# A two-layer graph network on one core: GpSimd's adding DMAs of the message stage become plain loads by SyncE, with the adds on VectorE and TensorE

## The chip, the cores and the metric

One core of one Trainium2 chip runs the whole program. The metric is the device time of one execution in microseconds (us). Five engines work side by side, each through its own instruction stream in order: TensorE (PE in the profile, its weight loads PEld), VectorE (DVE), ScalarE (ACT), GpSimd (POOL) and SyncE (SP), which here only starts DMAs.

## The reference

There are 100,000 nodes with 64 numbers each and 25,000 edges sorted by their target `dst`, each with a source `src` and 32 numbers of its own.

```
h   = relu(layernorm(x))
# layer 1: attention over the edges of a target, then batch norm over all nodes
score = sum(h[src] * h[dst]);  a = softmax of score over the edges of one dst
agg = segment_sum((h @ W_conv + b_conv)[src] * a, dst)
r   = relu(h @ W_res + b_res)
x2  = x + batchnorm(agg + r) * gamma + beta
# layer 2
h2  = relu(layernorm(x2))
m   = gelu(gelu([h2[src], h2[dst], edge_attr] @ W_m1 + b_m1) @ W_m2 + b_m2)
box = segment_sum(m, dst)
out = x2 + h2 + gelu(gelu([h2, box] @ W_c1 + b_c1) @ W_c2 + b_c2)
```

## The kernel before

The work runs in three stages. Stage A takes the nodes in 49 steps (2048 rows, one tile of 128 x 1024) and the edges in 49 groups (512 edges, 128 partitions with EJ = 4 edges each), computes `r` for all nodes and, for each edge, `r` of its two ends (`edge_r`), and stores them. Stage B makes `x2` and the final rows of all nodes as if no edge ended in them; meanwhile GpSimd gathers `agg` at the source of every edge (`gather_agg`) into a ring of RS = 4 tiles `agg_ring`, and SyncE stores each gathered tile to HBM (`stash_agg`, into `edge_agg`). Stage C, which the change is about, goes over the 49 groups again: it rebuilds `x2` of both ends of each edge, computes the messages, sums them by target and overwrites the rows of the targets (`put_final`).

A tile of a group in stage C is 128 x 512: four edges per partition, for each the 64 numbers of `dst` (side 0) and of `src` (side 1). The steps for group g, with the engine and the line of the group's main instruction:

- SyncE loads `edge_r` into `rr[g % 6]` (`load_edges`, L499), the row of flags that says whether an edge has the target of the one before (`load_prev`, L426), and the edge numbers (`load_attr`, L505, into one of four slots of `attr`).
- GpSimd adds `edge_agg` into side 1 of `rr` with a DMA that adds (`add_agg`, L625). VectorE multiplies the tile by the batch norm's scale (`scale_r`, L981). GpSimd adds `edge_x` with a second such DMA (`add_x`, L631).
- TensorE transposes `agg` of the targets (`fill_transpose`, L1504), VectorE carries it from the first edge of a target to its others with a scan (`fill_scan`, L990), and TensorE brings `rr` through the identity (L1516) and the scan through `fill_b` (L1519) into one PSUM bank: that sum is `x2` (`sum_edges`).
- VectorE subtracts the mean (`edge_x2`, L764 and L766), ScalarE squares, VectorE sums the squares of a pair of groups (L756), inverts both deviations in nine small operations (L694 to L702) and forms `h2` and `x2 + h2` (`edge_h2`, L770 and L1007).
- TensorE transposes `h2` (`transpose_pair`, L1530) and computes message layer 1 (`message1`, L1540 and L1542) and 2 (`message2`, L1549); VectorE sums messages by target with a scan (`message_scan`, L1016); TensorE computes the last two layers (`edge_c` L1556, `pair_out` L1567) and transposes back (`pair_back`, L1578); VectorE adds (`edge_final`, L1024); GpSimd scatters the rows (`put_final`, L591, four scatters per group).

The order is written out by hand, in iterations of a pair of groups. With a = 2i and b = a + 1, iteration i of each engine is:

- TensorE: transpose_pair(a-2), edge_c(a-4), message1(a-2), transpose_pair(a-1), edge_c(a-3), message2(a-2), message1(a-1), pair_out, sum_edges(a+2), fill_transpose(a+3), message2(a-1), pair_back, sum_edges(a+3), fill_transpose(a+4).
- VectorE: message_scan(a-4), edge_x2(a), edge_final(a-6), message_scan(a-3), edge_x2(b), edge_final(a-5), scale_r(a+4), fill_scan(a+2), the sums of squares of both groups, the inversion, edge_h2(a), edge_h2(b), scale_r(a+5), fill_scan(a+3).
- SyncE: load_edges(a+6), load_edges(a+7), load_prev(a+4), load_prev(a+5), load_attr(a+4), load_attr(a+5), and as long as there are gathered tiles to store (i up to 10), stash_agg of two groups. `load_attr(g)` waits until message1(g-4) is done, since it writes that slot:

```
def load_attr(g):
    C_m1.done(sp, g - 4)
```

- GpSimd, per group: add_agg(g+2), add_x(g), gather_agg(g+26) for g up to 22, and from group 24 on up to two put_final. gather_agg(g) waits until stash_agg(g-4) has read the ring's slot.

Of the kernel before, what the change touches and what calls it, by code (L numbers as in the profile page):

```python
# [12 lines left out]
P = 128  # L13
# [30 lines left out]
FIRST_PUT = 30  # L44
EDGES_ONLY = (9, 16, 23)
MS = 8


class Stage:
# [37 lines left out]
def program(nc, t, out):  # L87
# [13 lines left out]
    with ExitStack() as ctx:  # L101
        def sb(name, shape, dt=F32):
            return ctx.enter_context(nc.sbuf_tensor(name, shape, dt))
# [7 lines left out]
        def stage(name, incs=1):  # L111
            return Stage(sem(name), incs)

        def slots(name, n, incs=16):
            return Slots([sem(f"{name}{q}") for q in range(n)], incs)
# [87 lines left out]
        pairT = [sq[q // 2][:, (q % 2) * EG:(q % 2 + 1) * EG] for q in range(4)]  # L203
        x_ring = [sb(f"x_ring{q}", [P, EC]) for q in range(2)] + [gout[0][:, 0:EC], gout[0][:, EC:2 * EC]] + xe
        agg_ring = [sb(f"agg_ring{q}", [P, EW]) for q in range(RS)]


        bncol = sb("bncol", [P, 2])
# [81 lines left out]
        B_st = slots("final_rows_stored", XB)  # L290

        C_ld = Slots(E_st.sems, before=G)
        C_ga = slots("gathered_agg_added", 4)
        C_x = slots("edge_x_added", 4)
        C_ea = slots("edge_attr_loaded", 4)
        C_sm = slots("same_prev_loaded", MS)
        C_ft = stage("agg_transposed")
        C_fs = stage("agg_filled")
        C_ra = stage("edge_r_scaled")
        C_as = stage("edge_x2_summed")  # L300
        C_xd = stage("dst_x2_copied")
        C_f = stage("edge_x2_centered", 2)
# [29 lines left out]
        def edges_of(g):  # L332
            return P if g < NG else PT
# [10 lines left out]
        def is_group(g):  # L344
            return 0 <= g < G
# [25 lines left out]
        def rows(a):  # L371
            return a.rearrange("p (r d) -> p r d", d=D)

        def side(a, k):
            return a.rearrange("p (j s d) -> p j s d", s=2, d=D)[:, :, k, :]
# [16 lines left out]
        def _(sp):  # L392
# [100 lines left out]
            def load_edges(g):  # L493
                C_as.done(sp, g - 6)
                if g < 6:
                    E_st.all_done(sp, G)
                    sp.wait_ge(E_stat.sem, E_stat.after(G - 1))
                p = edges_of(g)
                sp.dma_start(rr[g % 6][0:p, :], edge_r[g][0:p, :]).then_inc(C_ld.of(g), 16)  # L499

            def load_attr(g):
                C_m1.done(sp, g - 4)
                c = edges_of(g) * EJ
                q = (g % 4) * DE
                sp.dma_start(attr[q:q + DE, 0:c], eaT[:, g * EG:g * EG + c]).then_inc(C_ea.of(g), 16)  # L505
# [26 lines left out]
            for i in range(PAIRS + 2):  # L532
                a = 2 * i
                for s in (a + RB, a + RB + 1):
                    if is_step(s):
                        load_r(s)
                if i == PAIRS - 1:
                    for g in range(2):
                        load_prev(g)
                    for g in range(6):  # L540
                        if g < 4:
                            load_attr(g)
                        load_edges(g)
                for s in (a - 3, a - 2):
                    if is_step(s):
                        store_final(s)
                for s in (a - 5 + XB, a - 4 + XB):
                    if s >= XB and is_step(s):
                        load_rows(s)
                due = min(G, max(stashed, agg_groups(min(a - 2, S - 1)) - G))  # L550
                stash_agg(stashed, due)
                stashed = due

            for i in range(PAIRS + 1):
                a = 2 * i
                if i == 0:
                    for g in range(2, 4):
                        load_prev(g)
                for g, do in ((a + 6, load_edges), (a + 7, load_edges), (a + 4, load_prev), (a + 5, load_prev),
                              (a + 4, load_attr), (a + 5, load_attr)):  # L560
                    if is_group(g):
                        do(g)
                due = max(stashed, min(G, agg_groups(S - 1) - G + a + 3))
                stash_agg(stashed, due)
                stashed = due
# [5 lines left out]
        def _(pool):  # L571
# [42 lines left out]
            def gather_agg(g):  # L614
                p = edges_of(g)
                Y_st.done(pool, g - RS)
                waits_end()
                for j in range(EJ):
                    gather(agg_ring[g % RS][0:p, j * D:(j + 1) * D], agg_rows, idx_of(src_idx, g, j, p), G_a.of(g))

            def add_agg(g):
                p = edges_of(g)
                pool.wait_ge(C_ld.of(g), C_ld.after(g))
                pool.wait_ge(Y_st.of(g), Y_st.after(g))
                A.dma_start(side(rr[g % 6][0:p, :], 1), rows(edge_agg[g][0:p, :]), accum_op=ALU.add)\  # L625
                 .then_inc(C_ga.of(g), 16)

            def add_x(g):
                p = edges_of(g)
                C_ra.done(pool, g)  # L630
                A.dma_start(rr[g % 6][0:p, :], edge_x[g][0:p, :], accum_op=ALU.add).then_inc(C_x.of(g), 16)  # L631

            def add_h2(s):
                p = nodes_of(s)
                pool.wait_ge(B_h.sem, B_h.after(s))
# [29 lines left out]
                    if is_group(n - G):  # L665
                        gather_agg(n - G)
            ahead = agg_groups(S - 1) - G
            last = G - ahead
            put = 0
            for g in range(2):  # L670
                add_agg(g)
            for g in range(G):
                if is_group(g + 2):
                    add_agg(g + 2)
                add_x(g)
                if is_group(g + ahead):
                    gather_agg(g + ahead)
                if g == last:
                    B_st.all_done(pool, S)
                due = min(g - 9, 2 * (g - last))  # L680
                while put < due:
                    put_final(put)
                    put += 1
            while put < G:
# [4 lines left out]
        def _(dve):  # L689
# [287 lines left out]
            def scale_r(g):  # L977
                p = edges_of(g)
                here = rows(rr[g % 6][0:p, :])
                dve.wait_ge(C_ga.of(g), C_ga.after(g))  # L980
                V.tensor_tensor(here, here, cols(bn[0:p, 0, :], ER), ALU.mult).then_inc(C_ra.sem, 1)  # L981

            def fill_scan(g):
# [341 lines left out]
        def _(pe):  # L1325
# [181 lines left out]
            def sum_edges(g):  # L1507
                p = edges_of(g)
                to = bank(1 + g % 2)[0:p, :]
                C_f.done(pe, g - 2)  # L1510
                C_xd.done(pe, g - 2)
                if g == 0:
                    pe.wait_ge(B_ht.sem, B_ht.after(S - 1))
                    pe.wait_ge(s_fill, 6)
                pe.wait_ge(C_x.of(g), C_x.after(g))
                T.matmul(to, ident[0:p, 0:p], rr[g % 6][0:p, :], start=True, stop=False)  # L1516
                pe.wait_ge(C_fs.sem, C_fs.after(g))
                for j in range(EJ):
                    ins = T.matmul(to[:, j * P:(j + 1) * P], fillT[g % 2][0:D + 1, j:p * EJ:EJ], fill_b[:, :],  # L1519
                                   start=False, stop=(j == EJ - 1))  # L1520
                ins.then_inc(C_as.sem, 1)
# [179 lines left out]
```

## Time and profile before

| what | us |
|---|---|
| median of 3 runs | 1961.68 |
| lowest and highest of them | 1946.9, 1965.65 |
| span of the profiled execution (first to last instruction) | 1753.3 |
| PE, DVE, ACT, POOL busy in the span | 1375.6, 1361.7, 833.2, 1363.7 |

The span is the profiled execution's own time as far as the profile shows it; the median of the runs lies 208.4 us above it, which is what surrounds the instructions. Stages A and B reach to about 1166 us of the span, stage C from there to the end. Where rows of the trace are shown below, a time is in us from the start of the span, and a row that merges several instructions gives their count after an x.

### The profile page before, as it was taken

How to read it: one execution, taken by the hardware profiler on the slowest of the kernel's cores; microseconds unless marked ns; L12 is line 12 of the kernel's file. 1: busy time of each engine (PE TensorE's matmuls, PEld its weight loads, DVE VectorE, ACT ScalarE, POOL GpSimd, SP SyncE). 2: the span in 40 equal slices, each digit the busy share in tenths (PEclk: the TensorE clock that was granted, in tenths of full speed). 3: DMA queues.
4: the chain of work that ended last, by engine and by line, in shares of the span. 5: the costliest groups of instructions: out<-in, count | busy, mean ns of one | idle time of the engine just before them, and what ended most of it. 6: DMA issues, size and time to landing. Idle time of an engine off the chain costs nothing.

```text
span 1753.3 us, 21724 instructions
## 1 busy us (share of the span) xinstructions
PE 1375.6 (78%) x6521; PEld 942.1 (54%) x6521; DVE 1361.7 (78%) x2229; ACT 833.2 (48%) x1448; POOL 1363.7 (78%) x1135
## 2 busy tenths in 40 slices
PE   3487777777776776988999889858889988787993
PEld 1266666666555564766667666634445444343541
DVE  8899899989877858898889888825767766555871
ACT  4655455545543435776668666621333432332441
POOL 7777777778777778788888887675767768888676
PEclk9788889888887877898889888955888987886987
DMA  7788776545543363444545565545656554545520
GB/s 210 249 283 290 282 264 219 165 145 157 161 150 96 106 224 102 157 166 166 201 162 186 174 200 178 160 98 108 121 120 124 118 117 97 107 89 98 122 48 18
DMA packets 154342, 273.55 MB, mean 156 GB/s; under 512 B 58386, under 2 KB 69361, under 8 KB 154228
## 3 DMA queue, kind: packets, MB, share of 16 engines
q1 hardware_dynamic: 71144, 183.91, 31.1%
q0 software_dynamic: 68112, 49.85, 16.7%
q10 hardware_dynamic: 14972, 38.41, 5.9%
q8 instruction: 54, 0.88, 0.2%
q14 instruction: 60, 0.49, 0.1%
HBM read 151.68 MB, written 121.80 MB: 156 GB/s over the span
## 4 chain that ended last, share of the span: by engine, by line
POOL 40%; issue 20%; DVE 18%; PE 13%; DMA 6%; ACT 2%; SPq 0%; POOLq 0%; DVEq 0%; ACTq 0%
POOL agg_rows L591 11%; POOL out L591 10%; POOL agg_ring L587 7%; DVE stat L756 4%; POOL xt L637 3%; DVE stat L764 3%; POOL part L587 3%; DMA rr<-edge_x 3%; DMA edge_agg<-agg_ring 2%; POOL rr L631 2%; DVE xc L770 1%; PE banks L1350 1%; DVE sums L821 1%; PE banks L1542 1%; PE banks L1540 1%
## 5 line engine op out<-in xcount | busy, mean ns | idle before, releaser
L587 POOL DMA_INDIRECT agg_ring<-agg_rows,edge_idx x196 | 233.2, 1190 | 112.2 <-DMA edge_agg<-agg_ring 57.2
L591 POOL DMA_INDIRECT agg_rows<-agg,put_first x196 | 234.0, 1194 | 55.9 <-issue 54.7
L587 POOL DMA_INDIRECT part<-in_x,edge_idx x192 | 217.3, 1132 | 58.5 <-issue 58.2
L591 POOL DMA_INDIRECT out<-agg,put_last x196 | 212.0, 1082 | 59.6 <-issue 59.6
L1335 PE MATMUL banks<-ident,xc 128*128 128x128 f32 (+1 forms) x784 | 135.1, 322 | 141.6 <-DVE xc L770 140.9
L1466 PEld LDWEIGHTS banks<-packed,cT 97*128 97x128 f32 (+1 forms) x1568 | 210.4, 218 | 45.3 <-issue 44.3
L1466 PE MATMUL banks<-packed,cT 97*128 97x64 f32 (+1 forms) x1568 | 218.6, 303 | 0.5 <-ACT cT L1198 0.5
L1335 PEld LDWEIGHTS banks<-ident,xc 128*128 128x128 f32 (+1 forms) x784 | 113.3, 177 | 152.0 <-DVE xc L770 130.8
L1456 PE MATMUL banks<-hT,packed 64*96 64x512 f32 (+1 forms) x392 | 125.5, 718 | 47.6 <-ACT cT L1198 43.0
L1081 ACT ACTIVATE hT<-banks 128x512 f32<-128x512 f32 (+1 forms) x98 | 55.4, 595 | 205.7 <-PE banks L1335 204.3
L587 POOL DMA_INDIRECT x_ring<-in_x,edge_idx x104 | 121.4, 1167 | 34.2 <-issue 34.2
L1516 PE MATMUL banks<-rr,ident 128*128 128x512 f32 (+1 forms) x98 | 69.2, 795 | 86.7 <-DMA rr<-edge_x 86.7
L587 POOL DMA_INDIRECT gout<-in_x,edge_idx x96 | 111.3, 1159 | 29.3 <-issue 29.3
L981 DVE TENSOR_TENSOR rr<-rr,bn 128x512 f32<-128x512 f32 (+1 forms) x49 | 33.9, 692 | 122.0 <-DMA rr<-edge_agg 122.0
L756 DVE TENSOR_REDUCE stat<-sq 128x16 f32<-128x1024 f32 (+1 forms) x98 | 117.1, 1212 | 14.6 <-ACT sq L1073 14.6
L1073 ACT ACTIVATE sq<-xc 128x1024 f32<-128x1024 f32 (+1 forms) x98 | 102.9, 1050 | 52.6 <-DVE xc L766 52.3
L1350 PE MATMUL banks<-hT,packed 128*128 128x512 f32 (+1 forms) x196 | 119.1, 739 | 1.3 <-ACT hT L1081 1.3
L766 DVE SCALAR_TENSOR_TENSOR xc<-stat,xt 128x1024 f32<-128x1024 f32 (+1 forms) x86 | 117.6, 1368 | 3.0
L770 DVE SCALAR_TENSOR_TENSOR xc<-xc,stat 128x1024 f32<-128x1024 f32 (+1 forms) x98 | 117.1, 1217 | 1.7
L1519 PEld LDWEIGHTS banks<-fill_b,sums 65*128 65x128 f32 (+1 forms) x392 | 99.0, 326 | 32.0 <-issue 19.1
L764 DVE TENSOR_REDUCE stat<-xt 128x16 f32<-128x1024 f32 (+1 forms) x86 | 104.1, 1210 | 14.3 <-POOL xt L637 6.1
L1257 ACT ACTIVATE sq<-banks 128x512 f32<-128x512 f32 (+1 forms) x49 | 28.9, 590 | 177.0 <-PE banks L1530 173.2
(163 smaller groups left out, 3351.2 us busy)
## 6 DMA issues: line engine op xcount, KB each, us to landing
xt<-in_x SPq DMA_DIRECT2D x84, 512.0 KB, 5.2
r_rows<-rT ACTq DMA_DIRECT2D x48, 512.0 KB, 5.4
agg_rows<-rb SPq DMA_DIRECT2D x48, 512.0 KB
out<-xt SPq DMA_DIRECT2D x36, 512.0 KB, 3.0
edge_r<-rr ACTq DMA_DIRECT2D x48, 256.0 KB, 5.0
rT<-r_rows SPq DMA_DIRECT2D x24, 512.0 KB, 6.5
part<-r_rows SPq DMA_DIRECT2D x24, 512.0 KB, 6.9
rr<-edge_r SPq DMA_DIRECT2D x48, 256.0 KB, 3.2
```

Source lines behind the costliest of these rows:

```text
L587: A.indirect_dma_start(to, None, table[:, :], bass.IndirectOffsetOnAxis(ap=idx, axis=0), bounds_check=limit, oob_is_err=False).then_inc(si ...
L591: A.indirect_dma_start(table[:, :], bass.IndirectOffsetOnAxis(ap=idx, axis=0), rows_of, None, bounds_check=limit, oob_is_err=False).then_i ...
L756: V.tensor_reduce(total, rows(squares), AX, ALU.add).then_inc(st.sem, 1)
L764: V.tensor_reduce(total, rows(source), AX, ALU.add).then_inc(st.sem, 1)
L766: V.scalar_tensor_tensor(out=rows(tile), in0=per_row(total), scalar=-1.0 / D, in1=rows(source), op0=ALU.mult, op1=ALU.add).then_inc(st.sem, 1)
L770: V.scalar_tensor_tensor(out=tile, in0=source, scalar=0.0, in1=per_row(deviation), op0=ALU.max, op1=ALU.mult).then_inc(st.sem, 1)
L1073: A.activation(sq[s % 2][0:p, :], xc[s % CS][0:p, :], ACT.Square).then_inc(st.sem, 1)
L1335: ins = T.transpose(to[:, c:c + p], xc[s % CS][0:p, c:c + P], ident[0:p, 0:p])
L1350: T.matmul(blocks(W[0][:, c], p), wres2[:, :], blocks(hT[:, c], p), start=True, stop=True)\
L1456: ins = T.matmul(blocks(bank(4 + i)[0:H2, :], p), wc1_node[i * D:i * D + D, :], blocks(hT[i * D:i * D + D, b * HALF:(b + 1) * HALF], p), s ...
L1466: ins = T.matmul(to[0:p, i * D:i * D + D], cT[b][:, i % 2, (i // 2) * P:(i // 2) * P + p], wc2[:, :], start=(i == 0), stop=(i == 7))
L1519: ins = T.matmul(to[:, j * P:(j + 1) * P], fillT[g % 2][0:D + 1, j:p * EJ:EJ], fill_b[:, :], start=False, stop=(j == EJ - 1))
```

## The change

`add_agg` and `add_x` leave GpSimd's stream. SyncE loads `edge_agg` into a new ring `agg_in` of MI = 4 tiles and `edge_x` into four tiles that stage A used (`x_in`); both are plain DMAs. `scale_r` gets a VectorE add of `agg_in` into side 1 of `rr` ahead of its multiply. `sum_edges` gets another product with the identity, so that `x_in` and `rr` are added in PSUM. SyncE's iteration is now load_edge_x(a+4), load_agg(a+4), load_edges(a+6), load_edge_x(a+5), load_agg(a+5), load_edges(a+7), and then load_prev, load_attr and stash_agg as before. GpSimd does the remaining gathers one after the other, with a put_final behind each from the eleventh on, and then the other put_final.

```diff
+MI = 4
+FINALS_BEHIND = 10
...
+        agg_in = [sb(f"agg_in{q}", [P, EW]) for q in range(MI)]
+        x_in = x_ring[0:MI]
...
+            def load_edge_x(g):
+                C_as.done(sp, g - MI)
+                if g == 0:
+                    X_st.all_done(sp, G)
+                    sp.wait_ge(E_ctr.sem, E_ctr.after(G - 1))
+                elif g == 2:
+                    sp.wait_ge(B_fin.sem, B_fin.after(S - 1))
+                p = edges_of(g)
+                sp.dma_start(x_in[g % MI][0:p, :], edge_x[g][0:p, :]).then_inc(C_x.of(g), 16)
+
+            def load_agg(g):
+                C_ra.part(sp, g - MI, 1)
+                p = edges_of(g)
+                sp.wait_ge(Y_st.of(g), Y_st.after(g))
+                sp.dma_start(agg_in[g % MI][0:p, :], edge_agg[g][0:p, :]).then_inc(C_ga.of(g), 16)
...
+                        if g < MI:
+                            load_agg(g)
+                        if g < 2:
+                            load_edge_x(g)
...
                 if i == 0:
+                    for g in range(2, MI):
+                        load_edge_x(g)
                     for g in range(2, 4):
                         load_prev(g)
-                for g, do in ((a + 6, load_edges), (a + 7, load_edges), (a + 4, load_prev), (a + 5, load_prev),
+                for g, do in ((a + 4, load_edge_x), (a + 4, load_agg), (a + 6, load_edges), (a + 5, load_edge_x),
+                              (a + 5, load_agg), (a + 7, load_edges), (a + 4, load_prev), (a + 5, load_prev),
                               (a + 4, load_attr), (a + 5, load_attr)):
...
             ahead = agg_groups(S - 1) - G
-            last = G - ahead
             put = 0
-            for g in range(2):
-                add_agg(g)
-            for g in range(G):
-                if is_group(g + 2):
-                    add_agg(g + 2)
-                add_x(g)
-                if is_group(g + ahead):
-                    gather_agg(g + ahead)
-                if g == last:
+            for g in range(ahead, G):
+                gather_agg(g)
+                if g == ahead:
                     B_st.all_done(pool, S)
-                due = min(g - 9, 2 * (g - last))
-                while put < due:
+                if g - ahead >= FINALS_BEHIND:
                     put_final(put)
                     put += 1
...
             def scale_r(g):
+                to = side(rr[g % 6][0:p, :], 1)
+                dve.wait_ge(C_ld.of(g), C_ld.after(g))
                 dve.wait_ge(C_ga.of(g), C_ga.after(g))
+                V.tensor_tensor(to, to, rows(agg_in[g % MI][0:p, :]), ALU.add).then_inc(C_ra.sem, 1)
+                dve.wait_ge(C_ra.sem, C_ra.after(g, 1))
                 V.tensor_tensor(here, here, cols(bn[0:p, 0, :], ER), ALU.mult).then_inc(C_ra.sem, 1)
...
                 pe.wait_ge(C_x.of(g), C_x.after(g))
-                T.matmul(to, ident[0:p, 0:p], rr[g % 6][0:p, :], start=True, stop=False)
+                T.matmul(to, ident[0:p, 0:p], x_in[g % MI][0:p, :], start=True, stop=False)
+                pe.wait_ge(C_ra.sem, C_ra.after(g))
+                T.matmul(to, ident[0:p, 0:p], rr[g % 6][0:p, :], start=False, stop=False)
```

## Rows read from the trace of the kernel before

**Rows 1.** Busy time of a stretch: PE, PEld, DVE, ACT, POOL, then PEclk, DMA share, GB/s
```profile
1500.00:1550.00 50.00, 40.24 (x118) 19.98 (x118) 27.11 (x50) 15.01 (x26) 40.79 (x39) 0.80 0.46 92
```

**Rows 2.** Timeline of POOL: start, duration, engine and line
```profile
1501.69 1.34 POOL L625 DMA_DIRECT2D rr<-edge_agg  x1
...
1514.85 1.34 POOL L625 DMA_DIRECT2D rr<-edge_agg  x1
```

**Rows 3.** Timeline of PE, behind a wait
```profile
1533.91 2.04 PE L1516 MATMUL banks<-rr,ident 128*128 128x512 f32 x2 [4.38 <-DMA rr<-edge_x]
...
1540.68 1.08 PE L1540 MATMUL banks<-attr,packed 32*80 32x512 f32 x2
```

**Rows 4.** Chain of waits in stage C, about 1246 us
```profile
1245.56 1.03 PE banks L1542 x2
1246.98 2.68 DMA edge_agg<-agg_ring
```

**Rows 5.** Who waited for whom, SyncE's queue, stage C
```profile
SPq L505 <- PE banks L1542: 427.7, 45, 20.5
```

**Rows 6.** Timeline of SyncE's queue
```profile
1263.59 0.90 SPq L521 DMA_DIRECT2D edge_agg<-agg_ring  x2
...
1643.04 0.90 SPq L499 DMA_DIRECT2D rr<-edge_r  x2
```

**Rows 7.** Timeline of PE, one pair of groups
```profile
1641.55 1.09 PE L1542 MATMUL banks<-sq,packed 128*80 128x512 f32 x2
...
1643.58 1.13 PE L1516 MATMUL banks<-rr,ident 128*128 128x512 f32 x2
1644.54 1.90 PE L1519 MATMUL banks<-fill_b,sums 65*128 65x128 f32 x8
...
1649.26 1.90 PE L1519 MATMUL banks<-fill_b,sums 65*128 65x128 f32 x8
...
1651.44 0.60 PE L1530 MATMUL banks<-ident,part 128*128 128x128 f32 x4
...
1658.16 1.08 PE L1542 MATMUL banks<-sq,packed 128*80 128x512 f32 x2
```

**Rows 8.** Timeline of DVE, the same pair
```profile
1637.69 0.68 DVE L981 TENSOR_TENSOR rr<-rr,bn 128x512 f32<-128x512 f32 x1
1638.29 1.27 DVE L990 TENSOR_TENSOR_SCAN sums<-rb,sums,banks 64x512 f32<-64x512 f32 x1
...
1641.43 0.69 DVE L756 TENSOR_REDUCE stat<-esq 128x8 f32<-128x512 f32 x1 [0.68 <-ACT esq L1111]
...
1644.04 0.69 DVE L770 SCALAR_TENSOR_TENSOR part<-part,stat 128x512 f32<-128x512 f32 x1
...
1646.17 0.68 DVE L981 TENSOR_TENSOR rr<-rr,bn 128x512 f32<-128x512 f32 x1
```

**Rows 9.** DMA issues of stage C: KB each, median us from issue to landing
```profile
rr<-edge_r SPq DMA_DIRECT2D x42, 256.0 KB, 3.1
...
rb<-prev_row SPq DMA_DIRECT2D x22, 256.0 KB, 4.6
...
edge_agg<-agg_ring SPq DMA_DIRECT2D x22, 128.0 KB, 2.1
```

**Rows 10.** Timeline at the stage's head: DVE's last of stage B, PE's first sum
```profile
1165.47 1.23 DVE L949 TENSOR_TENSOR xt<-xt,gout 106x1024 f32<-106x1024 f32 x1 [10.83 <-ACT gout L1206]
...
1187.75 2.23 PE L1519 MATMUL banks<-fill_b,sums 65*128 65x128 f32 x8 [0.95 <-DVE sums L990]
```

**Rows 11.** Timeline at its end: PE's last sum, DVE's last add, POOL's last scatters
```profile
1700.65 1.62 PE L1519 MATMUL banks<-fill_b,sums 65*106 65x128 f32 x8
...
1725.09 0.42 DVE L1024 TENSOR_TENSOR agg<-banks,agg 106x256 f32<-106x256 f32 x1 [2.95 <-PE banks L1578]
...
1739.57 0.97 POOL L591 DMA_INDIRECT out<-agg,put_last  x1 [0.30 <-issue]
...
1746.47 1.55 POOL L591 DMA_INDIRECT out<-agg,put_last  x1 [0.30 <-issue]
```

More of the change, by code:

```diff
@@ L292, in program @@
         C_ld = Slots(E_st.sems, before=G)
-        C_ga = slots("gathered_agg_added", 4)
-        C_x = slots("edge_x_added", 4)
+        C_ga = slots("gathered_agg_loaded", MI)
+        C_x = slots("edge_x_loaded", MI)
         C_ea = slots("edge_attr_loaded", 4)
@@ L298, in program @@
         C_fs = stage("agg_filled")
-        C_ra = stage("edge_r_scaled")
+        C_ra = stage("edge_r_scaled", 2)
         C_as = stage("edge_x2_summed")
@@ L619, in gather_agg @@
                     gather(agg_ring[g % RS][0:p, j * D:(j + 1) * D], agg_rows, idx_of(src_idx, g, j, p), G_a.of(g))
[L621 to L631, printed above, removed]
             def add_h2(s):
```

## The prediction, on record before the result

> **What bounds the kernel now.** I read the busy time by stretch first, then the chain of waits, then the timelines of single engines. Stage C is where the change acts. From its first sum to its last it takes 1700.65 - 1187.75 = 512.9 us [rows 10, 11]: TensorE's iterations 0 to 23, 24 spacings of a pair of groups, 21.4 us a pair on average. Two regimes lie in it. Around 1500 to 1550 GpSimd is the bound: busy 40.8 of 50 us while TensorE still shows idle time at a mean clock of 0.80 [rows 1], and one group takes 13.16 us from one add_agg to the next [rows 2], that is two adding DMAs and eight scatters. Around 1650 TensorE is the bound: its instructions follow one another without a wait, and a pair takes 1658.16 - 1641.55 = 16.61 us at full clock [rows 7]. Earlier still, the chain passes from message1 on TensorE to a stash by SyncE [rows 4]: the third party is SyncE, which stood 427.7 us in 45 waits at load_attr for message1 (L1542) [rows 5]. It costs little so far, since what stands behind that wait, the load of edge_r, is six groups ahead of need.
>
> **What goes away.** The two adding DMAs leave GpSimd: in 13.16 us of the GpSimd regime eight scatters of 0.97 + 0.30 us [rows 11] are 10.2 us, so the adds are some 3 us a group. What is left per pair where gathers and scatters alternate is 16 indirect DMAs of about 1.3 us, 21 us. The GpSimd bound of 26 us a pair is gone, if nothing takes its place.
>
> **What is added and costs nothing by itself.** The second identity product is 0.96 us a group (from L1516 to L1519) [rows 7]; it makes TensorE's pair 16.6 + 1.9 = 18.5 us. VectorE's add of 128 x 256 is 0.42 us by the add of nearly that shape [rows 11], with 0.04 us, an estimate of the hand-over between two instructions that depend on each other, scale_r is 1.06 us to the next instruction where it was 1638.29 - 1637.69 = 0.60 [rows 8]. SyncE gets four more issues a pair, 0.45 us each by two in 0.90 [rows 6].
>
> **What takes the place: a ring through SyncE.** load_agg(a+4) stands in SyncE's iteration i behind load_attr(a+3) of the iteration before, and that waits for message1(a-1). message1(a-1) is late in TensorE's iteration i. But VectorE's iteration i has scale_r(a+4) in its middle, ahead of fill_scan(a+2), the squares, the inversion and h2 of both groups. Before, `edge_r` was loaded six groups ahead and the adds were GpSimd's, so nothing in VectorE's iteration i hung on message1(a-1). Now it does: scale_r was at 1637.69 [rows 8], five us ahead of the end of message1(a-1) at 1641.55 + 1.09 = 1642.64 [rows 7]. Queued behind the waiting VectorE is all that TensorE's iteration i+1 starts from. I follow the ring once round, from 1642.64, at full clock:
>
> - SyncE: load_attr 0.40 (its next issue is at 1643.04 [rows 6]), load_edge_x and load_agg 0.90; in 10 of the iterations two stashes before them, 0.90 more. Issued 1.3 us (2.2) on.
> - The load's landing: no row shows one of 128 KB from HBM. A store of 128 KB takes 2.1, a load of 256 KB 3.1, the widest 4.6 us [rows 9]. I take 3.0, near the load, because 256 KB of `x_in` go ahead of it; both ends, 2.1 and 4.6, go into the range. Sum 4.3 (5.2).
> - scale_r(a+4) 1.06, then fill_scan(a+2) 1.27 + 0.04, squares 1.4 (two of 0.69), inversion 1644.04 - 1642.12 = 1.9, h2 of both groups 1646.17 - 1644.04 = 2.13, scale_r(a+5) 1.06, fill_scan(a+3) 1.27 [rows 8] and 0.06 to TensorE: 10.2.
> - TensorE, held for fill_scan(a+3) in the second sum: 1651.44 - 1649.26 = 2.18 to transpose_pair, and from there to the end of the next iteration's last message1 1659.24 - 1651.44 = 7.80 [rows 7]: 9.98.
>
> Together 24.5 us, 25.4 with stashes, 24.9 on average over the 22 iterations (1 to 22) in which the ring turns. TensorE's other work of the pair lies beside it: it waits some 3.8 us in sum_edges(a+2) for fill_scan (ready 6.7 us after message1, its two identity products done at 2.9), works 5.8 us, and waits 2.0 us in sum_edges(a+3). So the new product is hidden at no cost by these waits; without them it would be 1.9 us a pair.
>
> **The clock.** A wait of 4.38 us is followed by products at half clock, 2.04 us for what takes 1.13 [rows 3, 7], and the regime with such waits has a mean of 0.80 [rows 1]. That wait was followed by 6.8 us at 1.2 GHz: at 1540.68 a pair of products takes 1.08 us again, which is 2.4 GHz [rows 3]. 6.8 us at half clock are 3.4 us lost; 2.0 of them fit into the second wait, 1.4 come on top. The pair is 24.9 + 1.4 = 26.3 us.
>
> By the Trainium skill, "DMA: Bandwidth & Descriptors", section "Anatomy of one DMA — SWDGE (gpsimd) path", a DMA costs about 2.0 us and its bytes over 436e3, which for 128 KB is an estimate of 2.3 us; with it in place of 3.0 the ring would be 0.7 us shorter, 15 us over the stage. The rows' own 2.1 and 3.1 enclose it.
>
> **Head and end.** Before, the first sum came 21.1 us after VectorE's last final row (1166.70) [rows 10], through adding DMAs. Now agg, `edge_r` and x of the first groups land during stage B; VectorE does four scale_r (4.2) and a scan (1.27): first sum at 1172.3, 15.4 us earlier. At the end GpSimd finished 22.9 us after the last final add (1725.09 + 0.42 to 1748.02) [rows 11], with scatters queued. From empty it would be four scatters, 5.1 us; but the last finals still come faster than the 5.1 us that a group's scatters take, so of 0 to 17 us I take 5. Iterations 0 and 23 run at TensorE's 18.5, near 20 with some half clock.
>
> **Sum.** 22 x 26.3 = 579, and 2 x 20 = 40: 619 us against 512.9, +106. Less 15.4 and 5: +85 us. The span 1753.3 becomes 1839; with the 208.4 us around it, which the median of the runs has over the profiled span, 2047 us.
>
> **The bounds.** Low: landing 2.1 instead of 3.0 and no loss of clock, 22 x 24.0 + 37 = 565; +52, less 15 and 17: +20, 1982. High: landing 4.6 (+1.6), and a half clock for 40% of the pair as in the GpSimd regime, 11 us with 5.6 lost of which 2.0 are hidden (3.6 instead of 1.4): 22 x 30.1 + 40 = 702; +189, less 15 and 5: +169, 2131; both together are rare, I cut at 2115.
>
> **Rivals.**
> *Faster: the loads are there in time, and TensorE is the bound.* For it: GpSimd is free, and each adding DMA stood in the chain. Then a pair is 18.5 at full clock (24 x 18.5 = 444) to 20.5 (492): -69 to -21, and head and end 20 more, 1872 to 1921; middle 1897. A page gives a ground for it: the same page, section "SWDGE vs HWDGE vs iDMA", sends plain transfers to SyncE and only adding ones to GpSimd, since the hardware path sets up faster. Against it: it needs load_agg issued some 5 + 4 us earlier than the order of SyncE's stream allows, whatever the latency of one load. Chance 0.10, for a wait that I misread.
> *No change:* the ring turns but VectorE makes up part of it, so that a pair is 22.3 us: 22 x 22.3 + 40 = 531, +18 less 20, 1960. It would take a ring 4 us shorter than the rows give. Chance 0.03.
> *Slower than my range: the half clock takes the ring's TensorE part.* If all 9.98 us of it run at 1.2 GHz, a pair is 34.9 us: 22 x 34.9 + 40 = 808, +295 less 20, 2237. It decides only if each wait is followed by over 15 us at half clock; rows 3's was not. Chance 0.05, with all that lies between 2115 and there.
> *The change not doing what it says* would be GpSimd still bound by its 21 us a pair: below 26.3, so it decides only within the faster rival.
>
> **Chances.** Forecast 0.82, faster rival 0.10, no change 0.03, slower still 0.05. The range must drop no more than 0.2: 1982 to 2115 leaves out the outer cases. A measurement of this kernel tells about 1% (20 us) from no change. Faster by over 1%: 0.10; within 1%, with the lowest edge of the forecast: 0.04; slower: 0.86.
>
> **What would show it.** Right: VectorE waits once per pair, ahead of the new add, for the DMA from `edge_agg`, 5 to 8 us each time; the SyncE rows of that load follow a message1 (L1542's place) by 1 to 2 us; PE sums come every 26 us from the second pair to the last but one, with no long wait for `edge_x`; GpSimd is idle for a good part of stage C. The head's first sum is near 1172. Wrong: if VectorE's wait is absent, the order in SyncE's stream doesn't bind and the time falls under 1920; if pairs take 26 us but from TensorE waiting on x, the ring is another. A landing far from 3.0 us or a clock far from 0.8 moves the size, at 22 us per us.

## The result, and the profile after

The changed kernel takes 2046.19 us (median of 4 runs, 2033.73 to 2051.33) where the kernel before takes 1954.29 (4 runs). The ratio is 1.0433, 95% interval 1.0356 to 1.051: slower. Ratios and their intervals, here and below, are worked out from the fast runs of both kernels and aren't quotients of the medians, which give 1.047 here. A second measurement on another chip gives 2049.26 us and a ratio of 1.0383 (1.0287 to 1.0479).

One thing has to be said first, since the spans can't be compared without it. The profiled execution after has a span of 2049.3 us in a run of 2051.33: only 2 us lie around the instructions. The span of 1753.3 us that the prediction started from isn't 208 us of surroundings short of the runs; it is an execution that was quicker ahead of stage C. A second profile of the kernel before (before_again, below) has a span of 1947.8 us in a run of 1949.91, and its stage C is that of the first profile. The quicker kind also occurs in timed runs: on one chip the kernel before takes 1744.95 us. So the comparison of stages uses before_again.

The page after, part 1:

```profile
span 2049.3 us, 22017 instructions
...
PE 1479.5 (72%) x6619; PEld 981.6 (48%) x6619; DVE 1378.1 (67%) x2278; ACT 832.2 (41%) x1448; POOL 1221.7 (60%) x1037
```

GpSimd's busy time fell to 1221.7 us, from 1363.7 in the first profile of before and 1339.1 in before_again, and the kernel became slower. The bounds of stage C come from the first and last start of two lines each, the product that ends a sum and VectorE's final rows of stage B. First the kernel after:

```profile
L1532 PE MATMUL banks<-fill_b,sums x392: 274/397/603, 1397.7 to 2002.1; 65*128 65x128 f32 x192, 65*106 65x128 f32 x4
...
L956 DVE TENSOR_TENSOR xt<-xt,gout x37: 1210/1217/3556, 910.7 to 1391.1; 128x1024 f32<-128x1024 f32 x36, 106x1024 f32<-106x1024 f32 x1
```

and before_again:

```profile
L1519 PE MATMUL banks<-fill_b,sums x392: 274/397/602, 1378.2 to 1894.0; 65*128 65x128 f32 x192, 65*106 65x128 f32 x4
...
L949 DVE TENSOR_TENSOR xt<-xt,gout x37: 1210/1217/3549, 884.1 to 1356.2; 128x1024 f32<-128x1024 f32 x36, 106x1024 f32<-106x1024 f32 x1
```

From first to last sum it is 604.4 us after and 515.8 before: +88.6. The head, from the start of the last final row to the first sum, is 6.6 us against 22.0: -15.4. The end, from the last sum to the span's end, is 47.2 against 53.8: -6.6. Stage C costs 66.6 us more. The wait table of stage C after says where:

```profile
DVE rr L990 <- DMA agg_in<-edge_agg: 199.3, 21, 14.4
POOL out L618 <- DVE agg L1035: 188.7, 14, 19.3
...
PE banks L1532 <- DVE sums L1001: 82.4, 21, 9.3
```

The rows give the total, the number of waits and the longest. VectorE stood 199.3 us in 21 waits for the load of `edge_agg`; TensorE then stood 82.4 us for fill_scan (L1001); GpSimd, the bound of one part of the stage before, now waits 188.7 us for finals (the rows of the targets that it scatters). SyncE's queue spent its time where the prediction put it:

```profile
SPq L525 <- PE banks L1555: 355.2, 30, 24.2
```

One turn of the ring can be read in three timelines. TensorE, from one message1(a-1), whose last line is L1555, to the next (they answer to [rows 7]):

```profile
1638.97 1.09 PE L1555 MATMUL banks<-sq,packed 128*80 128x512 f32 x2
...
1641.00 1.13 PE L1527 MATMUL banks<-x_ring,ident 128*128 128x512 f32 x2
1641.96 1.02 PE L1529 MATMUL banks<-rr,ident 128*128 128x512 f32 x2
1647.00 2.24 PE L1532 MATMUL banks<-fill_b,sums 65*128 65x128 f32 x8 [4.02 <-DVE sums L1001]
...
1654.55 1.87 PE L1529 MATMUL banks<-rr,ident 128*128 128x512 f32 x2
1656.26 1.90 PE L1532 MATMUL banks<-fill_b,sums 65*128 65x128 f32 x8
...
1658.43 0.60 PE L1543 MATMUL banks<-ident,part 128*128 128x128 f32 x4
...
1665.16 1.08 PE L1555 MATMUL banks<-sq,packed 128*80 128x512 f32 x2
```

SyncE, which issues as soon as L1555 is done at 1640.06:

```profile
1635.77 4.66 SPq L525 DMA_DIRECT2D attr<-in_edge_attr_t  x2
1640.47 0.92 SPq L541 DMA_DIRECT2D edge_agg<-agg_ring  x2
1641.43 0.45 SPq L513 DMA_DIRECT2D gout<-edge_x  x1
1641.98 0.41 SPq L519 DMA_DIRECT2D agg_in<-edge_agg  x1
```

and VectorE (they answer to [rows 8]):

```profile
1644.61 0.42 DVE L990 TENSOR_TENSOR rr<-rr,agg_in 128x256 f32<-128x256 f32 x1 [8.89 <-DMA agg_in<-edge_agg]
1645.07 0.69 DVE L992 TENSOR_TENSOR rr<-rr,bn 128x512 f32<-128x512 f32 x1
1645.68 1.26 DVE L1001 TENSOR_TENSOR_SCAN sums<-rb,sums,banks 64x512 f32<-64x512 f32 x1
...
1653.24 1.27 DVE L1001 TENSOR_TENSOR_SCAN sums<-rb,sums,banks 64x512 f32<-64x512 f32 x1
```

The reader sees message1 end at 1640.06, the load issued 1.9 us later, the add 4.55 us after message1 behind 8.89 us of waiting, both scans behind it, the transposes of the next iteration at 1658.43 and the next message1's end at 1666.24: 26.2 us for a pair. The spacings of every second L1532, worked out from the timeline of the whole stage, are 24.1 to 30.5 us in iterations 1 to 22, 25.9 on average; before, they were 16.6 to 28.4. The 30.5 is iteration 22, whose load for the last group, of 106 partitions, was issued at 1968.65 and reached the add 8.8 us later.

### The profile page after: what moved, and what is told of

It reads as the page before. It is cut to its first block, busy times and chain, and to the rows that moved or that the text cites. A ratio compares the mean times of both kernels' runs of the same rounds, so it can differ in the third digit from the quotient of the medians.

```text
span 2049.3 us, 22017 instructions
## 1 busy us (share of the span) xinstructions
PE 1479.5 (72%) x6619; PEld 981.6 (48%) x6619; DVE 1378.1 (67%) x2278; ACT 832.2 (41%) x1448; POOL 1221.7 (60%) x1037
## 4 chain that ended last, share of the span: by engine, by line
issue 27%; PE 23%; DVE 18%; POOL 16%; another core or an unknown queue 9%; DMA 3%; ACT 2%; SPq 1%; DVEq 0%; POOLq 0%; ACTq 0%
POOL agg_rows L618 9%; DVE stat L763 3%; DVE stat L771 3%; PE banks L1532 3%; POOL xt L652 3%; PE banks L1477 2%; POOL agg_ring L614 2%; DMA agg_in<-edge_agg 2%; PE banks L1361 2%; PE banks L1562 2%; DVE sums L1001 2%; PE banks L1346 2%; PE banks L1555 2%; PE banks L1467 1%
## 5 line engine op out<-in xcount | busy, mean ns | idle before, releaser
L618 POOL DMA_INDIRECT out<-agg,put_last x196 | 202.8, 1034 | 245.7 <-DVE agg L1035 188.7
L614 POOL DMA_INDIRECT part<-in_x,edge_idx x192 | 208.8, 1088 | 117.2 <-DVE part L773 59.9
L1346 PE MATMUL banks<-ident,xc 128*128 128x128 f32 (+1 forms) x784 | 141.8, 332 | 151.6 <-DVE xc L777 102.1
L1346 PEld LDWEIGHTS banks<-ident,xc 128*128 128x128 f32 (+1 forms) x784 | 118.5, 183 | 165.9 <-DVE xc L777 92.9
L1361 PE MATMUL banks<-hT,packed 128*128 128x512 f32 (+1 forms) x196 | 134.7, 819 | 78.5 <-ACT hT L1092 50.7
L1532 PE MATMUL banks<-fill_b,sums 65*128 65x128 f32 (+1 forms) x392 | 101.3, 418 | 98.0 <-DVE sums L1001 82.4
L990 DVE TENSOR_TENSOR rr<-rr,agg_in 128x256 f32<-128x256 f32 (+1 forms) x49 | 20.6, 421 | 218.7 <-DMA agg_in<-edge_agg 199.3
L652 POOL TENSOR_TENSOR xt<-xt,xc 128x1024 f32<-128x1024 f32 (+1 forms) x37 | 93.7, 2532 | 117.8 <-DVE xc L777 117.4
L1532 PEld LDWEIGHTS banks<-fill_b,sums 65*128 65x128 f32 (+1 forms) x392 | 97.0, 326 | 133.3 <-DVE sums L1001 102.1
L614 POOL DMA_INDIRECT gout<-in_x,edge_idx x96 | 101.1, 1053 | 56.1 <-issue 27.7
L1287 ACT ACTIVATE part<-banks,packed 64x512 f32<-64x512 f32 (+1 forms) x49 | 33.3, 681 | 232.4 <-PE banks L1562 149.0
```

The lines of the kernel that those rows point to most:

```text
L614: A.indirect_dma_start(to, None, table[:, :], bass.IndirectOffsetOnAxis(ap=idx, axis=0), bounds_check=limit, oob_is_err=False).then_inc(si ...
L618: A.indirect_dma_start(table[:, :], bass.IndirectOffsetOnAxis(ap=idx, axis=0), rows_of, None, bounds_check=limit, oob_is_err=False).then_i ...
L652: A.tensor_tensor(here, here, xc[s % CS][0:p, :], ALU.add).then_inc(B_y.sem, 1)
L1346: ins = T.transpose(to[:, c:c + p], xc[s % CS][0:p, c:c + P], ident[0:p, 0:p])
L1361: T.matmul(blocks(W[0][:, c], p), wres2[:, :], blocks(hT[:, c], p), start=True, stop=True)\
```

## The experiments

"Sums" is the time from first to last start of the product that ends a sum, read as above. A ratio is to the kernel before on the same chip; the chips differ, as the column shows, so ratios and sums are to be compared, not times across rows. Every profile is one execution.

| kernel | us | before there | ratio (95%) | sums us |
|---|---|---|---|---|
| before_again | 1949.91, one run | 1968.35 | | 515.8 |
| changed | 2046.19 | 1954.29 | 1.0433 (1.0356 to 1.051) | 604.4 |
| after_again | 2049.26 | 1983.82 | 1.0383 (1.0287 to 1.0479) | 604.9 |
| x_only | 1962.24 | 1968.35 | 0.9963 (0.982 to 1.0105) | 493.2 |
| agg_only | 2017.06 | 1968.35 | 1.0301 (1.0189 to 1.0413) | 569.7 |
| agg_late | 1938.21 | 1744.95 | 1.1111 (1.1031 to 1.1191) | 722.3 |
| attr_later | 1912.59 | 1968.35 | 0.967 (0.9504 to 0.9837) | 494.7 |
| attr_later2 | 1930.03 | 1983.82 | 0.9742 (0.9627 to 0.9857) | 494.6 |
| agg_ring6 | 1656.01 | 1744.95 | 0.951 (0.9452 to 0.9568) | 440.9 |
| gathers_paced | 1653.98 | 1744.95 | 0.949 (0.9433 to 0.9548) | 440.9 |
| gathers_paced2 | 1970.91 | 1986.4 | 0.9872 (0.9732 to 1.0013) | 514.7 |
| x_on_vector | 1917.03 | 1983.82 | 0.9725 (0.9634 to 0.9816) | 466.3 |
| x_on_vector_paced | 1945.84 | 1986.4 | 0.9831 (0.9729 to 0.9934) | 494.6 |

What lies ahead of stage C differs between executions by as much as some of these effects: on one chip the last final row of stage B starts at 1356.2 us in before_again and at 1367.9, 1375.6 and 1401.6 us in attr_later, agg_only and x_only. The sums are the sharper reading of the ring.

**The order alone: attr_later.**

```diff
-                              (a + 4, load_attr), (a + 5, load_attr)):
-                    if is_group(g):
+                              (a + 2, load_attr), (a + 3, load_attr)):
+                    if is_group(g) and not (do is load_attr and g < 4):
```

> Only the order of SyncE's stream differs from the changed kernel: load_attr(a+2) and load_attr(a+3) stand in iteration i in place of load_attr(a+4) and load_attr(a+5), so what is queued behind the wait for message1 is released one pair earlier. Ring theory: load_agg(a+4) is issued before VectorE needs it, the 9 to 11 us waits ahead of the new add vanish, a pair of groups takes 18.5 to 21 us instead of 25, first to last sum 450 to 500 us instead of 604, the kernel 1900 to 1950 us. Rival (the added work itself, a second product and four more loads a pair, is what costs): nothing is taken away here, so 2020 to 2060 us as the changed kernel.

The waits ahead of the new add fell from 199.3 us in 21 to this:

```profile
  DMA agg_in<-edge_agg: 1.1, 1
```

and where nothing else stalls, TensorE works without a gap at full clock (stretch, length, PE, PEld, DVE, ACT, POOL, PEclk, DMA share, GB/s):

```profile
1700.00:1800.00 100.00, 100.00 (x351) 52.16 (x351) 86.06 (x163) 39.45 (x69) 47.13 (x43) 1.00 0.39 117
```

Its pairs take 18.3 us (L1532 at 1666.43 and 1684.76), four of the first ten 28 to 36, of which more below. Same instructions, same transfers, only the place of load_attr in the order changed: the kernel is faster than the changed one and than before (the interval of its ratio lies wholly under 1). The cause of the slowdown is shown: the wait that stands ahead of the load in SyncE's stream. The second run of this kernel agrees.

> The reordered kernel once more. In the first look four of its first ten pairs took 28 to 36 us, 54 us more than 18.3 each, with waits whose cause the profile doesn't name. On a chip without such waits it should equal the ring of six: first to last sum 441 us, 1650 to 1660 us where before takes 1745, ratio 0.95. If the waits belong to its dense stream of indirect DMAs: 490 us again.

It met its second case: sums of 494.6 us again, on another chip of the slower kind. The changed kernel beside it:

> The changed kernel once more, beside its repairs on the same chip. On a chip where the kernel before takes about 1745 us (stage A then ends near 685 us instead of 885) the ring theory gives the same difference in stage C: first to last sum 600 us against 514, pairs of 25 us, so 1820 to 1840 us, and a ratio of 1.045 to 1.055; on a chip like the first, 2046. Rival (the stalls seen around stage A also make stage C's pairs long): pairs well under 25 us on the quick chip.

604.9 us of sums, and the slowdown a second time.

**The distance: agg_ring6.** The order of load_attr stays, agg is asked for one pair earlier.

```diff
+MA = 6
...
-                for g, do in ((a + 4, load_edge_x), (a + 4, load_agg), ...
-                              (a + 5, load_agg), ...
+                for g, do in ((a + 4, load_edge_x), (a + 6, load_agg), ...
+                              (a + 7, load_agg), ...
```

(`agg_in` gets six tiles; load_attr's signals reuse four that stage A is done with.)

> The changed kernel with the order of load_attr left alone, but a ring of six agg_in tiles and load_agg(a+6) and (a+7) in iteration i, so that agg is asked for one pair earlier, still behind the same wait for message1. Ring theory: it is the distance that counts, so the wait ahead of the new add goes as with attr_later: pairs of 18.3 us where nothing else stalls, first to last sum 480 to 510 us, the kernel 1890 to 1940 us. Rival (SyncE's blocked stream delays edge_x and edge_r as well, and agg was only the first to show): pairs of 21 to 25 us with TensorE waiting for edge_x, 1950 to 2020 us.

440.9 us of sums, better than expected, since the chip showed none of the unnamed stalls; all but one of its pairs from the third on take 17.8 to 18.3 us, that one 22.7. No wait of VectorE for agg is left in its table, and none of TensorE for `edge_x` carries weight. The rival, that `edge_x` would be the next to come late, fell: it is used an iteration later than agg.

**The dose: agg_late.** The two load_agg stand behind load_prev instead of ahead of load_edges.

> The changed kernel with load_agg(a+4) and load_agg(a+5) moved behind load_edges, load_edge_x and load_prev in the same iteration of SyncE's stream. It issues the first of them some 2.3 to 3 us later (five more DMAs of 0.45 us, and 1.3 MB more ahead of it in the queues, 2 to 6 us at 200 to 250 GB/s). Ring theory: every us of delay is paid once a pair, 22 times: 4 to 8 us more a pair, first to last sum 690 to 780 us, the kernel 2130 to 2230 us. Rival (the pair is bound by work and clock, the load is hidden in part): less than 30 us more than the changed kernel's 2046.

SyncE's queue and VectorE's wait:

```profile
1551.49 0.42 SPq L513 DMA_DIRECT2D x_ring<-edge_x  x1
...
1554.38 0.85 SPq L519 DMA_DIRECT2D agg_in<-edge_agg  x2
```
```profile
1560.00 0.42 DVE L990 TENSOR_TENSOR rr<-rr,agg_in 128x256 f32<-128x256 f32 x1 [14.48 <-DMA agg_in<-edge_agg]
```

The load is issued 2.9 us after the first of the block, where it was 0.55 in the changed kernel, and is added 5.6 us after its issue (5.4 us to land is the median), where it was 2.6. That is 5.3 us more in the turn shown. The sums are 722.3 us, 118 more than the changed kernel's, which is 5 us for each of the 22 to 23 turns; pairs take 29.3 to 32.8 us. The changed kernel was not run on this chip, so the two sums come from chips of different kinds. The kernel took 1938.21 us only because its chip has before at 1744.95; the 193 us over it would be 2148 on the first chip, inside the expected 2130 to 2230. A us in this load is a us in each pair.

**The two halves.** x_only keeps add_agg as GpSimd's DMA, agg_only keeps add_x.

```diff
 x_only, against before:
-                add_x(g)
...
-                T.matmul(to, ident[0:p, 0:p], rr[g % 6][0:p, :], start=True, stop=False)
+                T.matmul(to, ident[0:p, 0:p], x_in[g % MI][0:p, :], start=True, stop=False)
...
+                T.matmul(to, ident[0:p, 0:p], rr[g % 6][0:p, :], start=False, stop=False)
 agg_only, against before:
-                if is_group(g + 2):
-                    add_agg(g + 2)
...
+                V.tensor_tensor(to, to, rows(agg_in[g % MI][0:p, :]), ALU.add).then_inc(C_ra.sem, 1)
```

> The x half of the change alone: SyncE loads edge_x, TensorE adds it with the identity; agg is still added by GpSimd's DMA in the order of before. Ring theory: no ring through agg, since GpSimd issues it; TensorE bound of 18.5 us a pair, and GpSimd has one adding DMA of 1.7 us a group less, so first to last sum 470 to 510 us against 513 of before, the kernel 1900 to 1960 us. Rival (the loads of edge_x behind SyncE's wait for message1, or the second product, cost the time): 2000 to 2050 us, with TensorE waiting for edge_x.

> The agg half of the change alone: SyncE loads edge_agg, VectorE adds it; edge_x is still added by GpSimd's DMA. Ring theory: the ring is whole, and edge_x's adding DMA of 5 us now follows scale_r, so a pair takes 24 to 28 us, first to last sum 590 to 650 us, the kernel 2030 to 2090 us, with VectorE waiting for the load from edge_agg once a pair. Rival (the x half costs): near the kernel before, 1930 to 1980 us.

x_only is level with before (0.9963, the interval holds 1): 493.2 us of sums, inside the expected range, while its time of 1962 us lies just over the expected 1960. So the load of `edge_x` behind SyncE's wait and the second product don't account for the slowdown. agg_only has the slowdown, ratio 1.0301, with the same wait:

```profile
DVE rr L983 <- DMA agg_in<-edge_agg: 184.3, 22, 12.1
```

Its 569.7 us of sums lie under the expected 590, and it missed the expected time too: its pairs take 22.8 to 24.7 us in the steady part, but for one of 27.6, on average some 1.5 us less than the changed kernel's. Most of it is the way to the add. A turn with stashes, message1 ending at 1616.14 us:

```profile
1617.54 0.40 SPq L507 DMA_DIRECT2D agg_in<-edge_agg  x1
```
```profile
1619.79 0.42 DVE L983 TENSOR_TENSOR rr<-rr,agg_in 128x256 f32<-128x256 f32 x1 [7.73 <-DMA agg_in<-edge_agg]
```

Without the 256 KB of `edge_x` ahead of it the load is issued 1.4 us after message1 (1.9 in the changed kernel) and is added 2.25 us later (2.63), 0.9 us less together. Where the rest comes from, the missing second product among the candidates, was not separated.

**The waits without a name, and pacing GpSimd.** In attr_later ScalarE stands like this, the releaser being given as "remote", which here means that no event in the trace accounts for the end of the wait:

```profile
1415.81 0.60 ACT L1268 ACTIVATE sq<-banks 128x512 f32<-128x512 f32 x1 [30.78 <-remote]
```

GpSimd was issuing gathers one behind another in that time, until 1412.8 us. gathers_paced is attr_later with two more edits: gather_agg waits for the sum of an earlier group, and the finals no longer stand between the gathers.

```diff
-FINALS_BEHIND = 10
+FINALS_BEHIND = 30
...
             for g in range(ahead, G):
+                C_as.done(pool, g - ahead - 3)
                 gather_agg(g)
```

> attr_later with GpSimd's stream thinned out: gather_agg(26 + k) also waits for the sum of group k - 3, and no put_final stands between gathers. In attr_later four pairs of the first ten took 28 to 36 us instead of 18.3, with ScalarE and VectorE standing 3 to 31 us although what they wait for was done, while GpSimd issued indirect DMAs back to back. If that dense issue is what holds them: those stalls go, first to last sum 440 to 460 us, the kernel 30 to 50 us less than attr_later, 1860 to 1885 us, though 49 put_final of 5.1 us each then have to fit behind the last gather and may end it 10 to 20 us later. If the stalls come from elsewhere: sum 480 to 500 us as attr_later, 1910 to 1930 us.

> gathers_paced once more: its first run was on a chip where the kernel before takes 1745 us and where no wait without a named cause occurs at all, so it said nothing about them. If this chip is one where before takes 1950 to 1990 us and GpSimd's dense issue holds the others up, the stalls of attr_later's first ten pairs (54 us) go: first to last sum 441 to 455 us, 1865 to 1895 us. If they come whatever GpSimd does: 480 to 500 us, 1910 to 1930 us. On a quick chip: 441 us again, and the question stays open.

The first run says nothing on it: on the quick chip the table of waits names no "remote" for any kernel. The second run, on a chip where before takes 1986.4 us, is the answer, and it isn't the expected one (455 us of sums at most, or 480 to 500): 514.7 us, and the stalls moved. Pairs 3 to 11, with gathers spaced, take 17.8 to 18.3 us each, where attr_later lost 36 of its 54 us in three pairs. Pair 2, in which GpSimd still issues 20 gathers without a break, takes 33.3; and pairs 12 and 13 take 40.2 and 61.4 us, where GpSimd now puts its backlog of finals back to back (columns as above):

```profile
1500.00:1600.00 100.00, 100.00 (x355) 52.57 (x355) 86.14 (x157) 39.34 (x69) 54.66 (x46) 1.00 0.50 139
1600.00:1700.00 100.00, 61.38 (x169) 27.31 (x166) 38.17 (x76) 20.43 (x36) 77.46 (x75) 0.72 0.26 74
```
```profile
1641.41 0.60 ACT L1269 ACTIVATE sq<-banks 128x512 f32<-128x512 f32 x1 [12.14 <-remote]
```

In the second stretch GpSimd's 75 indirect DMAs of 1.03 us with 0.30 us between them fill the 100 us, and TensorE's busy time falls to 61. Such stalls come with GpSimd's unbroken runs, on these chips; on the quick chip 144 indirect DMAs followed one another unbroken from 1331.4 to 1537.3 us in gathers_paced and stalled nobody, its pairs taking 18.3 us all through. What holds the others during them stays open.

**x added on VectorE.** Against attr_later, with the waits left out:

```diff
                 V.tensor_tensor(here, here, cols(bn[0:p, 0, :], ER), ALU.mult).then_inc(C_ra.sem, 1)
...
+                V.tensor_tensor(here, here, rows(x_in[g % MI][0:p, :]), ALU.add).then_inc(C_ra.sem, 1)
...
-                T.matmul(to, ident[0:p, 0:p], x_in[g % MI][0:p, :], start=True, stop=False)
```

> The reordered kernel with edge_x added by VectorE (one more add of 128 x 512, 0.69 us a group, behind the multiply of scale_r) and the second identity product left out. TensorE's pair goes back from 18.3 to 16.6 us; VectorE's busy time a pair becomes 15.0 + 1.4 = 16.4 us, so both are near the bound. If VectorE's small waits don't add up: pairs of 16.6 to 17.2 us, first to last sum 405 to 420 us, 20 to 35 us less than the reordered kernel. If they do (its stream stands for ScalarE's squares 1.6 us a pair): pairs of 18 to 19 us, no gain or a loss of up to 20 us.

> x_on_vector with GpSimd's stream thinned as in gathers_paced. Its quiet pairs took 16.6 to 17.5 us, its first ten 22 on average. If the thinning works: first to last sum 415 to 425 us, 20 to 25 us less than gathers_paced2; if not, 460 to 470 us as x_on_vector. Its head is 11 us later than gathers_paced2's, since scale_r of groups 2 and 3 waits for the last rows of stage B.

The quiet pairs of x_on_vector take 16.5 to 17.5 us, with some of 19.2: between the two cases. Sums are 466.3 us, well over the expected 405 to 420 since the stalls are in its first ten pairs too, and 28 less than attr_later2's on the same chip, as expected. The head is 17.5 instead of 6.6 us; the ratio 0.9725 can't be told from attr_later2's 0.9742. With pacing it had two pairs of 35.4 and 60.0 us in the same place as gathers_paced2 and 494.6 us of sums: a miss.

**The second profile of before.**

> The kernel before once more, for a second profile of it, since the first has a span of 1753.3 us where the runs take 1942 to 1966 us. If executions differ ahead of stage C, this one shows the last final row of stage B near 1390 us instead of 1167, and stage C unchanged at 513 us from first to last sum. If the missing 200 us lie around the instructions, its span is near 1750 us again.

The last final row of stage B is at 1356.2 us (1390 expected), stage C is unchanged (515.8 against 514.1 us by the same reading), and the span is 1947.8. The extra 200 us are in stage A, whose table of waits has such lines, while the first profile's has none:

```profile
ACT hT L1081 <- remote: 144.8, 13, 39.5
DVE inv L832 <- remote: 130.1, 10, 41.5
```

## Why the prediction was right, and where it was not

The forecast was 2047 us, slower, by a ring through SyncE; the mechanism was the one found: attr_later removed it by order alone, agg_ring6 by asking earlier, and agg_late made it longer by what the load came later.

- *What bounds now.* The GpSimd bound of 26 us a pair did go, and nothing of the gain was left since a ring of the same length took its place, and took it in every pair, also in those that had taken 16.6 us.
- *The ring.* Forecast 24.9 us, 26.3 with the clock; measured 25.9 on average. By its steps, for the turn shown, one with stashes: message1 to the add 4.55 us (5.2 forecast: the landing was 2.6 from issue to add, not 3.0, and the issue 0.3 quicker); scale_r 1.07 (1.06); the scan, squares, inversion, h2, scale_r and scan to 1654.51 8.8 (9.1); TensorE from the second sum to message1 1666.24 - 1656.26 = 9.98 (9.98).
- *The waits that hide the product.* The first was 4.02 us (3.8 forecast). The second, forecast at 2.0, is not there: the scan was ready at 1654.51 and TensorE's identity products, at half clock, ran until 1656.26. The half clock took the second wait and 1.75 us more (1.4 forecast).
- *The signs.* VectorE's waits ahead of the new add were there, 21 of them, but 9.5 us on average where 5 to 8 were named. No wait of TensorE for `edge_x` stands in the table.
- *Sum from first to last.* Forecast 619, measured 604.4: 22 x 25.9 = 570 and the two outer pairs 12.7 + 21.1 = 34 instead of 2 x 20.
- *Head and end.* -15.4 forecast and -15.4 measured; -5 forecast and -6.6 measured. At the end GpSimd's last scatter again ended 19 us after the last final add, on finals that came faster than it scatters (before it was 22.5 us; the prediction's 22.9 counts from the add's start).
- *A premise that was wrong*: "208.4 us around it, which the median of the runs has over the profiled span". 2 us lie around the instructions; the rest was stage A, which took some 200 us longer in the timed runs than in the profiled one. Adding the constant was harmless, as it stood in both kernels. It did cost knowledge: stage A's unnamed waits were in the runs but not in the rows.
- *Its size.* The forecast was +85 us from 1961.68. By stage C it is +67 us; the ratios mean +85 (70 to 100) on the first chip and +76 (57 to 95) on the second, and the first chip's medians differ by 92. Of the 19 us that the forecast has too much in stage C, 9 are the 22 turns (579 against 570) and 6 the outer pairs; the remaining 4 or so come from the readings of before, the head and the end. So the agreement at 2046 is in part luck: the rest of the measured difference lies ahead of stage C, where the profiled executions on one chip differ by up to 45 us, and no run explains it.
- *The rivals.* The faster one is what attr_later and agg_ring6 are: 18.3 us a pair where 18.5 was worked out; what kept it away was the order of the stream, as the prediction says against it. The half clock over the whole ring did not come; the granted clock was 0.83 from first to last sum in the changed kernel, 0.82 in before_again. The Trainium skill, "DMA: Bandwidth & Descriptors", section "SWDGE vs HWDGE vs iDMA", which the prediction names for the faster rival, says that the hardware path sets up faster; its reason for the choice of engine is what the transfer does (plain, or adding), not the speed. Here 256 KB landed 3.1 us after the issue as SyncE's plain load and 5.1 us as GpSimd's adding DMA (medians before, stage C), and no run separates the path from the adding.
- *The landing.* The forecast took 3.0 us, and from issue to the add it was 2.63 us. By the Trainium skill, "DMA: Bandwidth & Descriptors", section "Anatomy of one DMA — SWDGE (gpsimd) path", the estimate was 2.3 us; that section's fit is for DMAs that GpSimd issues, and this load is SyncE's, so it was borrowed. The measurement lies between the two.

## What to carry to other kernels

When a transfer moves into an in-order queue, look at what the queue waits for just ahead of it, and follow that wait forward: if it hangs on the consumer's own iteration, a ring closes, and its length, not any engine's busy time, is the time of the loop wherever it is the longest of the bounds. Count in iterations how far ahead each load is issued, for every load that is moved; here six groups ahead was free, four cost 4%, and moving another load's wait by one pair turned the 4% into a gain of 3%. A cost that is off the path in the profile (the second product of 1.9 us a pair, hidden in the ring's waits) is paid when the ring is gone: 16.6 became 18.3, and 16.5 to 17.5 with the add on VectorE instead.

## What the runs showed of the hardware that was not expected

On most chips here the kernel before takes 1950 to 1990 us, on one 1745, with the same program. In the two profiles of before the difference is in stage A (VectorE's first final row of stage B starts at 884.1 and 685.7 us), where ScalarE and VectorE wait up to 41.5 us with no event in the trace to account for it; the first profile and those from the quick chip have no such line. In stage C such waits follow GpSimd's runs of indirect DMAs that are issued 0.3 us apart without a break: when the gathers were spaced and the finals bunched, the waits moved from the gathers to the finals.
